# An attention and feed-forward kernel: the squares of the hidden values folded once more by GpSimd, their column sums moved behind the third up chunk

## Chip, cores and metric

One core of one Trainium2 chip. The metric is the device time of one launch in microseconds (us), lower is better. Matmuls run on TensorE (PE), element-wise work on VectorE (DVE), ScalarE (ACT) and GpSimd (POOL), transfers are issued by SyncE (SP). Each engine takes its instructions strictly in program order, and the engines meet at semaphores that the kernel writes out by hand.

## What is computed

Sixteen batch entries of 256 rows by 256 columns go through an attention block and then a ternary-weight feed-forward block, each with a layer norm before and after and a residual:

```
x = x + _layernorm(attn(_layernorm(x)))
x = x + _layernorm(ffn(_layernorm(x)))

def ffn(x):                      # FF = 1024 hidden columns
    gate, up = split(x @ wq_gate_up.T)
    h  = silu(gate) * up
    hn = h * rsqrt(mean(h * h, axis=-1) + eps)     # rms norm
    return hn @ wq_proj.T
```

The outer layer norm divides by the deviation of its input, so the kernel never applies the rms factor. It multiplies the un-normed `h` with the projection and adds a floor, worked out from the row sums of `h * h`, to the variance of the result. Those row sums are what the change is about.

## The kernel before

The attention part takes most of the program: until about 870 us, 128 steps of two heads. The feed-forward part follows, and its first steps lie between the last attention steps. Everything the change touches is in the feed-forward part.

A *unit* is one batch entry (256 rows, two tiles of 128). A *step* of the feed-forward pipeline works on five units at once, told by `FLAG = dict(stats=0, norm=1, turn=1, up=2, sum=3, down=3, z=3, out=4)`. Call w the unit whose `up` is in this step. Then the step holds

- the statistics of the input of unit w+2 (`stats_x2` on DVE, L1555 and L1558; `invert_x2` on POOL, four small operations, L620 to L627),
- the input norm of w+1 (`norm_x2` on ACT, L1175, two halves), its transposes on PE (L969), and the split of the result into a high part (`x2_hi`, ACT L1209) and a low part (`x2_lo`, DVE L1617),
- the up projection of w in four chunks c = 0 to 3 (`up`, PE L910, 16 matmuls each, gate half then up half). Each chunk goes through `activate` (silu, ACT L1154), `multiply` (gate times up, DVE L1535), `high_hidden` (ACT L1161), `square_hidden` (ACT L1168) and `split_hidden` (the low part, POOL L613),
- the down projection of w-1 (`down`, PE L940, 32 matmuls), the sums of its squares, the statistics of its result (`stats_z`, DVE L1582, L1587) and `invert_z` (four small POOL operations, L634 to L640),
- the outer norm of w-2 (`norm_z`, ACT L1183, two halves), its residual addition (`add_x`, POOL L646) and the store.

The squares of a unit are a tile of 8 slices of 128 hidden columns by 256 rows. DVE adds them down: `add_squares(0)` (L1542) brings slices 0 to 3 to two, `add_squares(2)` slices 4 to 7 to two, and `sum_squares` (L1548) the rest to slices 0 and 1. PE then multiplies slices 0 and 1 with a column of ones (`sum_tiles`, L920: for each of the two row tiles one matmul per slice, four in the program, eight rows in the trace), and DVE makes the floor of the sums (`sum_floor`, L1564).

The order of work is the order in which each engine's `step` function writes it. For PE that is up chunk 0, up chunk 1, down, sums, up chunk 2, transposes of w+1, up chunk 3. For POOL it is split 0, `invert_x2`, split 1, `add_x`, `invert_z`, split 2, split 3. The first of the four operations of `invert_x2` waits for two things:

```
pool.wait_ge(x2_aggr, u * 2 * NT + 2 * NT)
at_least(pool, x2_norm, u * NT)
```

Here u is w+2, so the second line asks that all units up to w+1 be normed by ACT: the small tiles of the statistics exist once and would be overwritten. `multiply` of chunk 3 stands behind `add_squares(0)` on DVE, and `multiply` of chunk 1 behind `add_squares(2)`, `sum_squares` and `stats_x2`.

The semaphores that matter: `h_summed` counts finished `sum_squares`, `sum_ready` finished sums on PE, `z_floored` finished floors, `x2_lo_done` lets the next unit's `up` begin.

Of the kernel before, what the change touches and what calls it, by code (L numbers as in the profile page):

```python
# [68 lines left out]
FC = 2  # L69
# [13 lines left out]
def sandwich_kernel(nc, x, wq, wkv, wkvh, wg, wout, wgu, wproj, rope, out):  # L83
    ctx = ExitStack()
    with ctx:
# [43 lines left out]
        def carve(*shape):  # L129
# [156 lines left out]
            sem(k) for k in ("h_added", "h_summed", "sum_ready", "z_floored", "z_ready"))  # L286
        z_stats, z_aggr, z_eps, z_neg, z_inv, z_biased, z_norm, res_done = (
            sem(k) for k in ("z_stats", "z_aggr", "z_eps", "z_neg", "z_inv", "z_biased", "z_norm", "res_done"))
        tile_done = sem("tile_done")
        stored = [sem(f"stored{i}") for i in range(2)]  # L290

        block = ctx.enter_context(nc.Block())
# [128 lines left out]
        def _(sp):  # L421
# [86 lines left out]
            sp.wait_ge(res_done, BATCH - 1)  # L508
            sp.dma_start(out_rows[:, TILES - 2 * NT:TILES - NT, :], res[0]).then_inc(stored[0], 16)
            for t in range(NT):  # L510
                sp.wait_ge(*((tile_done, t + 1) if t < NT - 1 else (res_done, BATCH)))
                sp.dma_start(out_rows[:, TILES - NT + t, :], res[1][:, t, :]).then_inc(stored[1], 16)
            sp.wait_ge(stored[0], 16 * BATCH // 2)
            sp.wait_ge(stored[1], 16 * BATCH // 2 + 16)
# [3 lines left out]
        def _(pool):  # L518
# [123 lines left out]
            def add_x(u, i):  # L642
# [2 lines left out]
                at_least(pool, stored[i], (u - i) * 8)  # L645
                nc.gpsimd.tensor_tensor(res[i], zn[i], x_batch(u), ALU.add).then_inc(res_done, 1)  # L646

            def place_down(g0, s):

                c = place_at(g0, s, PLACE_POOL)  # L650
                if c is not None:
                    j = c - (CHUNKS - ET)
                    pool.wait_ge(wt_back, 16 * CHUNKS)
                    pool.wait_ge(q_ready, STEPS)
                    nc.gpsimd.tensor_copy(wpr_t[:, :, j * P:(j + 1) * P],
                                          w_final[c].bitcast(BF16).rearrange("p (f c) -> p f c", c=P)).then_inc(wpr_placed, 1)

            def step(u0, s):
                at = unit_at(u0, s, FLAG["up"])
                if at:  # L660
                    split_hidden(*at, 0)
                at = unit_at(u0, s, FLAG["stats"])
                if at:
                    invert_x2(at[0])
                at = unit_at(u0, s, FLAG["up"])
                if at:
                    split_hidden(*at, 1)
                at = unit_at(u0, s, FLAG["out"])
                if at and not last_unit(at[0]):
                    add_x(*at)  # L670
                at = unit_at(u0, s, FLAG["z"])
                if at:
                    invert_z(*at)
                at = unit_at(u0, s, FLAG["up"])
                if at:
                    split_hidden(*at, 2)
                    split_hidden(*at, 3)

            def batch(g0, par, steps):
                for s in range(steps):  # L680
# [35 lines left out]
        def _(pe):  # L716
# [228 lines left out]
            def step(u0, s):  # L945
                at = unit_at(u0, s, FLAG["up"])
                if at:
                    up(*at, 0)
                at = unit_at(u0, s, FLAG["up"])
                if at:  # L950
                    up(*at, 1)
                at = unit_at(u0, s, FLAG["down"])
                if at:
                    u, i = at
                    down(u, i)
                    if not last_unit(u):
                        pe.wait_ge(h_summed, u + 1)
                        sum_tiles(u, i, range(FC))
                at = unit_at(u0, s, FLAG["up"])
                if at:  # L960
                    up(*at, 2)
                at = unit_at(u0, s, FLAG["turn"])
                if at:
                    u, i = at
                    pe.wait_ge(x2_norm, u * NT + NT)
                    at_least(pe, x2_lo_done, u)
                    for k in range(ET):
                        for t in range(NT):
# [50 lines left out]
        def _(act):  # L1019
# [164 lines left out]
                                         scale=z_rstd[:, t:t + 1]).then_inc(z_norm, 1)  # L1184

            def step(u0, s):
                at = unit_at(u0, s, FLAG["out"])
                if at:
                    norm_z(*at)
                at = unit_at(u0, s, FLAG["up"])  # L1190
                if at:
                    activate(*at, 0)
                    high_hidden(*at, 0)
                    activate(*at, 1)
                    high_hidden(*at, 1)
                at = unit_at(u0, s, FLAG["norm"])
                if at:
                    norm_x2(*at)
# [72 lines left out]
        def _(dve):  # L1271
# [295 lines left out]
            def add_x(u, i, t):  # L1567

                dve.wait_ge(z_norm, u * NT + t + 1)
                if t == 0:  # L1570
                    dve.wait_ge(stored[i], (u - i) * 8)
                nc.vector.tensor_tensor(res[i][:, t, :], zn[i][:, t, :], x_batch(u)[:, t, :], ALU.add)\
                    .then_inc(tile_done if t < NT - 1 else res_done, 1)

            def stats_z(u, i):

# [3 lines left out]
                at_least(dve, z_biased, u)  # L1580
                for t in range(NT):
                    nc.vector.bn_stats(z_stat[:, t, :], Z_BANK[i][:, t * E:(t + 1) * E]).then_inc(z_stats, 1)  # L1582
                if not last_unit(u):
                    sum_floor(u, i)
                dve.wait_ge(z_stats, u * NT + NT)
                for t in range(NT):
                    nc.vector.bn_aggr(z_agg[:, t, :], z_stat[:, t, :]).then_inc(z_aggr, 2)  # L1587
# [1 line left out]
            def step(u0, s):  # L1589
# [31 lines left out]
                if at:  # L1621
                    add_squares(*at, 0)
                    multiply(*at, 3)

            def batch(g0, par, steps):
                if isinstance(g0, int) and g0 == 0:
# [127 lines left out]
```

## Time and profile before

| | |
|---|---|
| median of 3 runs | 1093.43 us (1093.08 to 1095.97) |
| time of the profiled execution | 1093.13 us |
| its span | 1091.3 us |
| PE busy | 1052.3 us, 96% |
| POOL busy | 928.1 us, 85% |
| DVE busy | 872.8 us, 80% |
| ACT busy | 861.5 us, 79% |

The span is what the profiler saw between the first and the last instruction; the launch time is 1.8 us longer. Busy shares are means over the whole program. The feed-forward part has its own pattern, which repeats from unit to unit, and is read from a stretch or a timeline of its own. A busy PE in these rows counts a matmul from its start to its modelled end, so neighbouring matmuls overlap. "Idle before" in brackets is the time in which an engine had nothing, and the name behind it is what ended it.

### The profile page before, as it was taken

What the parts mean: (1) busy time and instruction counts of PE and PEld (TensorE: products, weight loads), DVE (VectorE), ACT (ScalarE), POOL (GpSimd) and SP (SyncE); (2) the same over time, 40 slices, a digit from 0 to 9 for tenths busy, and PEclk for the clock granted to TensorE, in tenths of its full rate; (3) what the DMA queues carried; (4) which work ended last, traced back from release to release, by engine and by line L of the source; (5) the groups of instructions that cost most, each with busy time, mean ns of one, the idle gap of its engine ahead of it and who ended that gap; (6) DMA issues with size and microseconds to landing.
All of it is one profiled execution on the core that took longest, in us unless ns stands there. A gap on an engine that the chain in (4) does not pass through costs nothing.

```text
span 1091.3 us, 25312 instructions
## 1 busy us (share of the span) xinstructions
PE 1052.3 (96%) x8010; PEld 1006.2 (92%) x8010; DVE 872.8 (80%) x2870; ACT 861.5 (79%) x2386; POOL 928.1 (85%) x846
## 2 busy tenths in 40 slices
PE   6899999999999999999999999999999899999997
PEld 6798999899989998998999999999999799999997
DVE  6879889989998998899889988987877656666654
ACT  4787888888888888887888788888878666666674
POOL 4698999899989999998999899999899658777685
PEclk9999999999999999999999999999999999999999
DMA  7450211021112110221021112111130000000001
GB/s 264 163 167 29 59 42 59 22 68 60 47 34 59 61 39 31 59 61 46 24 70 58 40 38 71 41 40 59 30 117 21 2 1 21 20 21 20 21 20 39
DMA packets 35124, 58.57 MB, mean 54 GB/s; under 512 B 3136, under 2 KB 16000, under 8 KB 34688
## 3 DMA queue, kind: packets, MB, share of 16 engines
q1 hardware_dynamic: 34992, 56.96, 16.6%
q8 instruction: 64, 1.05, 0.4%
q14 instruction: 68, 0.56, 0.2%
HBM read 50.92 MB, written 9.18 MB: 55 GB/s over the span
## 4 chain that ended last, share of the span: by engine, by line
POOL 59%; PE 21%; issue 17%; ACT 1%; DVE 1%; POOLq 0%; DMA 0%; ACTq 0%; DVEq 0%
POOL arena L575 15%; POOL arena L607 14%; POOL arena L596 14%; POOL arena L585 13%; PE psum L910 11%; PE psum L940 5%; PE psum L721 1%; PE psum L920 1%; PE psum L969 1%; POOL arena L545 1%; POOL X L566 1%; POOLq L297 0%; PE psum L747 0%; POOL arena L552 0%; PE psum L826 0%
## 5 line engine op out<-in xcount | busy, mean ns | idle before, releaser
L607 POOL TENSOR_TENSOR arena<-arena 128x768 f32<-128x768 f32 x128 | 196.5, 1535 | 18.8 <-DVE arena L1419 17.5
L575 POOL TENSOR_TENSOR arena<-arena,tables 128x512 f32<-128x512 f32 x128 | 165.7, 1295 | 39.4 <-ACT arena L1090 39.1
L585 POOL TENSOR_TENSOR arena<-arena 128x512 f32<-128x512 f32 x128 | 188.7, 1474 | 10.0
L1432 DVE SCALAR_TENSOR_TENSOR pt_split<-psum,vh_col,pt_split 128x256 fp32r<-128x256 f32 (+1 forms) x512 | 176.9, 407 | 0.0
L596 POOL TENSOR_TENSOR arena<-arena 128x512 f32<-128x512 f32 x128 | 165.2, 1290 | 2.6 <-DMA arena<-kh_rows 1.7
L826 PE MATMUL psum<-arena 128*128 128x256 f32 x512 | 154.6, 384 | 8.4 <-POOL arena L585 8.4
L1101 ACT ACTIVATE arena<-arena 128x256 f32<-128x256 f32 x256 | 128.6, 502 | 32.3 <-DVE arena L1409 25.5
L721 PE MATMUL psum<-wo_hi,o_hi 128*128 128x256 f32 x512 | 152.7, 298 | 0.0
L721 PE MATMUL psum<-xt_hi,wq_hi 128*128 128x256 f32 x512 | 146.0, 285 | 0.0
L721 PE MATMUL psum<-xt_lo,wq_hi 128*128 128x256 f32 x512 | 144.9, 283 | 0.0
L721 PE MATMUL psum<-xt_hi,wq_lo 128*128 128x256 f32 x512 | 144.9, 283 | 0.0
L721 PE MATMUL psum<-wo_hi,o_lo 128*128 128x256 f32 x512 | 144.2, 282 | 0.0
L721 PE MATMUL psum<-wo_lo,o_hi 128*128 128x256 f32 x512 | 143.7, 281 | 0.0
L721 PE MATMUL psum<-pt_split,vals_hi 128*128 128x512 f32 (+1 forms) x512 | 142.0, 358 | 0.4 <-DVE wo_lo L1283 0.4
L1089 ACT ACTIVATE arena<-psum 64x512 f32<-64x512 f32 x128 | 76.2, 596 | 80.9 <-DVE arena L1394 78.9
L910 PE MATMUL psum<-xt_hi,wq_hi 128*128 128x256 f32 x512 | 128.4, 290 | 0.5 <-DVE xt_lo L1617 0.5
L910 PE MATMUL psum<-xt_lo,wq_hi 128*128 128x256 f32 x512 | 124.6, 281 | 0.0
L1119 ACT ACTIVATE pt_split<-psum,vh_col 128x256 fp32r<-128x256 f32 x256 | 120.9, 472 | 0.0
L613 POOL TENSOR_TENSOR wo_lo<-arena,wo_hi 128x512 fp32r<-128x512 f32 x64 | 88.9, 1397 | 27.1 <-ACT wo_hi L1161 27.0
L828 PEld LDWEIGHTS psum<-arena 128*128 128x128 f32 x512 | 97.4, 190 | 13.5
L1441 DVE TENSOR_TENSOR o_lo<-psum,o_hi 128x512 fp32r<-128x512 f32 x128 | 87.2, 681 | 25.7 <-ACT o_hi L1129 25.6
L1407 DVE CUSTOM_DVE_ANT_0 arena<-psum,mask 128x256 f32<-128x256 f32 x256 | 106.8, 417 | 0.6 <-issue 0.5
(170 smaller groups left out, 3508.1 us busy)
## 6 DMA issues: line engine op xcount, KB each, us to landing
arena<-kh_rows SPq DMA_DIRECT2D x127, 256.0 KB, 3.3
out<-spare SPq DMA_DIRECT2D x15, 256.0 KB, 2.1
arena<-w_rows SPq DMA_DIRECT2D x6, 512.0 KB, 4.7
X<-L_attn_Wout SPq DMA_DIRECT2D x1, 2048.0 KB, 14.5
X<-L_attn_x SPq DMA_DIRECT2D x1, 2048.0 KB, 13.0
arena<-L_attn_Wq SPq DMA_DIRECT2D x1, 1536.0 KB, 10.1
X<-L_attn_x SPq DMA_DIRECT2D x1, 1536.0 KB, 10.2
w_rows<-L_ffn_w_gate_up SPq DMA_DIRECT2D x3, 512.0 KB, 9.3
```

The costliest lines, as they stand in the source:

```text
L575: nc.gpsimd.tensor_tensor(swap, swap, spread, ALU.mult).then_inc(q_sined, 1)
L585: nc.gpsimd.tensor_tensor(q_rot[p % 2], q_cos[p % 2], q_swap[p % 2], ALU.add).then_inc(q_roped, 1)
L596: nc.gpsimd.tensor_tensor(k_head[p % 2], keys[par].unsqueeze(1).to_broadcast([P, HP, N]), kh_all[p % 4], ALU.mult).then_inc(k_scaled, 1)
L607: nc.gpsimd.tensor_tensor(tb, tb, r.unsqueeze(3).to_broadcast([P, HP, 3, P]), ALU.mult).then_inc(p_ready, 1)
L721: last = nc.tensor.matmul(o, a, b, start=start and i == 0, stop=stop and i == len(passes) - 1, skip_group_check=skip)
L826: nc.tensor.matmul(sj[:, 0:2 * P], q[:, j, P:N], kt[:, j, :], start=True, stop=True, skip_group_check=True)
L828: nc.tensor.matmul(sj[:, 2 * P:3 * P], q[:, j, 0:P], kt[:, j, 0:P], start=False, stop=True, skip_group_check=True).then_inc(s_ready, 1)
L910: last = nc.tensor.matmul(bank[c % 2 * 2 + half][:, j * N:(j + 1) * N], wgu_t[:, k, col:col + P], part[:, k, :], start=n == 0 and j == 0, ...
L1101: nc.scalar.activation(tb[:, j, 0:2 * P], tb[:, j, 0:2 * P], ACT.Exp, scale=-1.0, bias=nmax[p % 4][:, 2 * j:2 * j + 1], accum_out=rsum[p % ...
L1119: nc.scalar.activation(pt_hi[p % 2][:, j * N:(j + 1) * N], b[:, 0:N], ACT.Copy, scale=vh[:, 0, h:h + 1])
L1407: nc.vector.tensor_tensor_reduce(tb[:, j, 0:2 * P], S_BANK[j][:, 0:2 * P], mask[:, :], -1.0, -MASKED, ALU.add, ALU.min, nmax[p % 4][:, 2 * ...
L1432: last = nc.vector.scalar_tensor_tensor(pt_lo[p % 2][:, o], b[:, i], vh[:, t, h:h + 1], pt_hi[p % 2][:, o].bitcast(F32), ALU.mult, ALU.sub ...
```

## The change

The diff does five things to the feed-forward steps.

1. POOL gets `fold_squares`: it adds slice 1 of the squares to slice 0 (128x256 numbers), for all units but the last, behind the low part of chunk 1. It waits for `h_summed` and counts `h_folded`.
2. PE sums slice 0 alone (two matmuls instead of four), no longer behind `down` but behind up chunk 2 and ahead of the transposes, and waits for `h_folded`.
3. POOL's `add_x` moves behind the low part of chunk 2, and `invert_z` to the end of the step, except for the last unit.
4. ACT's `norm_z` moves from the start of the step to behind `high_hidden` of chunk 1.
5. DVE's `sum_floor` moves from inside `stats_z` to the end of the step. The stores of the last unit wait for a semaphore of their own.

```diff
+            def fold_squares(u, i):
+
+                pool.wait_ge(h_summed, u + 1)
+                nc.gpsimd.tensor_tensor(squares[i][:, 0, :], squares[i][:, 0, :], squares[i][:, 1, :], ALU.add)\
+                    .then_inc(h_folded, 1)
...
                 at = unit_at(u0, s, FLAG["up"])
                 if at:
                     split_hidden(*at, 1)
+                at = unit_at(u0, s, FLAG["sum"])
+                if at and not last_unit(at[0]):
+                    fold_squares(*at)
+                at = unit_at(u0, s, FLAG["z"])
+                if at and last_unit(at[0]):
+                    invert_z(*at)
+                at = unit_at(u0, s, FLAG["up"])
+                if at:
+                    split_hidden(*at, 2)
                 at = unit_at(u0, s, FLAG["out"])
                 if at and not last_unit(at[0]):
                     add_x(*at)
+                at = unit_at(u0, s, FLAG["up"])
+                if at:
+                    split_hidden(*at, 3)
                 at = unit_at(u0, s, FLAG["z"])
-                if at:
+                if at and not last_unit(at[0]):
                     invert_z(*at)
-                at = unit_at(u0, s, FLAG["up"])
-                if at:
-                    split_hidden(*at, 2)
-                    split_hidden(*at, 3)
...
                     down(u, i)
-                    if not last_unit(u):
-                        pe.wait_ge(h_summed, u + 1)
-                        sum_tiles(u, i, range(FC))
                 at = unit_at(u0, s, FLAG["up"])
                 if at:
                     up(*at, 2)
+                at = unit_at(u0, s, FLAG["sum"])
+                if at and not last_unit(at[0]):
+                    u, i = at
+                    pe.wait_ge(h_folded, u + 1)
+                    sum_tiles(u, i, (0,))
...
-                at = unit_at(u0, s, FLAG["out"])
-                if at:
-                    norm_z(*at)
                 at = unit_at(u0, s, FLAG["up"])
                 if at:
                     activate(*at, 0)
                     high_hidden(*at, 0)
                     activate(*at, 1)
                     high_hidden(*at, 1)
+                at = unit_at(u0, s, FLAG["out"])
+                if at:
+                    norm_z(*at)
...
                     add_squares(*at, 0)
                     multiply(*at, 3)
+                at = unit_at(u0, s, FLAG["z"])
+                if at and not last_unit(at[0]):
+                    sum_floor(*at)
```

The change adds 17 lines, so a line behind the first of them has a higher number in the changed kernel. In the rows of the order below, L613 and L620 to L646 are the same in both; L910, L920, L940 and L969 of before are L924, L934, L954 and L985 of the changed kernel.

POOL, one step of the pipeline before, from `invert_x2` on:

```order
L620 TENSOR_TENSOR arena<-arena,eps 128x2 [waits x2_norm,x2_aggr]
L622 TENSOR_TENSOR arena<-arena 128x2
L624 TENSOR_TENSOR arena<-arena,minus_half 128x2 [waits x2_eps]
L627 TENSOR_TENSOR arena<-arena 128x2 [waits x2_inv,x2_neg]
L613 TENSOR_TENSOR wo_lo<-arena,wo_hi 128x512 [waits ht_hi_done]
L646 TENSOR_TENSOR spare<-arena,X 128x512 [waits stored1,z_norm]
L634 TENSOR_TENSOR arena<-arena 128x2 [waits z_norm,z_aggr,z_floored]
L635 TENSOR_TENSOR arena<-arena 128x2
L637 TENSOR_TENSOR arena<-arena,minus_half 128x2 [waits z_eps]
L640 TENSOR_TENSOR arena<-arena 128x2 [waits z_inv,z_neg]
L613 TENSOR_TENSOR wo_lo<-arena,wo_hi 128x512 [waits ht_hi_done] x3
```

The same place in the changed kernel (L651 is the fold):

```order
L620 TENSOR_TENSOR arena<-arena,eps 128x2 [waits x2_norm,x2_aggr]
L622 TENSOR_TENSOR arena<-arena 128x2
L624 TENSOR_TENSOR arena<-arena,minus_half 128x2 [waits x2_eps]
L627 TENSOR_TENSOR arena<-arena 128x2 [waits x2_inv,x2_neg]
L613 TENSOR_TENSOR wo_lo<-arena,wo_hi 128x512 [waits ht_hi_done]
L651 TENSOR_TENSOR arena<-arena 128x256 [waits h_summed]
L613 TENSOR_TENSOR wo_lo<-arena,wo_hi 128x512 [waits ht_hi_done]
L646 TENSOR_TENSOR spare<-arena,X 128x512 [waits stored0,z_norm]
L613 TENSOR_TENSOR wo_lo<-arena,wo_hi 128x512 [waits ht_hi_done]
L634 TENSOR_TENSOR arena<-arena 128x2 [waits z_norm,z_aggr,z_floored]
L635 TENSOR_TENSOR arena<-arena 128x2
```

The fold stands behind the whole of `invert_x2` and the low part of chunk 1, and `add_x` and `invert_z` have moved down.

PE before, the end of `down`, the sums and the start of up chunk 2:

```order
L940 MATMUL psum<-wq_lo,wo_hi 128x256
L940 MATMUL psum<-wq_lo,wo_lo 128x256
L920 MATMUL psum<-ones,arena 128x1 [waits z_floored,h_summed]
L920 MATMUL psum<-ones,arena 128x1 x3
L910 MATMUL psum<-xt_hi0,wq_hi 128x256 [waits gate_silu]
L910 MATMUL psum<-xt_lo0,wq_hi 128x256
```

PE in the changed kernel, the end of up chunk 2 up to the start of chunk 3:

```order
L924 MATMUL psum<-xt_lo0,wq_hi 128x256
L934 MATMUL psum<-ones,arena 128x1 [waits z_floored,h_folded]
L934 MATMUL psum<-ones,arena 128x1
L985 MATMUL psum<-ident,arena 128x128 [waits x2_lo_done,x2_norm]
L985 MATMUL psum<-ident,arena 128x128 x3
L924 MATMUL psum<-xt_hi0,wq_hi 128x256 [waits gate_silu]
L924 MATMUL psum<-xt_lo0,wq_hi 128x256
```

The sums are half as many, wait for another semaphore, and now stand directly ahead of the transposes.

## Rows read from the trace of the kernel before

**Rows 1.** Windows: busy time of each engine, granted clock, DMA share, GB/s.

```profile
980.00:1020.00 40.00, 40.00 (x332) 39.42 (x332) 25.02 (x53) 27.53 (x53) 28.60 (x40) 1.00 0.06 21
```

**Rows 2.** Chain that ended last, sums, up chunk 2, transposes: start us, us.

```profile
982.39 0.79 PE psum L920 x8
983.17 2.03 PE psum L910 x16
985.20 0.44 PE psum L969 x4
```

**Rows 3.** Waits, 900 to 1060 us: waiter, releaser, us in total, times, longest.

```profile
POOL arena L620 <- ACT arena L1175: 26.6, 12, 2.4
...
PEld psum L910 <- DVE xt_lo L1617: 2.9, 12, 0.5
```

**Rows 4.** Timeline, one step of the repeating pattern: start us, us, engine, line.

```profile
987.33 1.29 POOL L646 TENSOR_TENSOR spare<-arena,X 128x512 f32<-128x512 f32 x1
987.40 1.76 DVE L1542 TENSOR_TENSOR arena<-arena 128x512 f32<-128x512 f32 x1
...
989.08 0.67 DVE L1535 TENSOR_TENSOR arena<-arena,psum 128x512 f32<-128x512 f32 x1
...
989.79 0.63 ACT L1161 ACTIVATE wo_hi<-arena 128x512 fp32r<-128x512 f32 x1 [1.24 <-DVE arena L1535]
...
990.85 1.00 ACT L1183 ACTIVATE arena<-psum,arena 128x256 f32<-128x256 f32 x2
991.75 0.60 ACT L1154 ACTIVATE arena<-psum 128x512 f32<-128x512 f32 x1
992.38 0.69 DVE L1535 TENSOR_TENSOR arena<-arena,psum 128x512 f32<-128x512 f32 x1 [2.62 <-ACT arena L1154]
...
995.39 0.69 DVE L1535 TENSOR_TENSOR arena<-arena,psum 128x512 f32<-128x512 f32 x1
...
996.11 0.63 ACT L1161 ACTIVATE wo_hi<-arena 128x512 fp32r<-128x512 f32 x1 [1.90 <-DVE arena L1535]
996.65 1.08 ACT L1175 ACTIVATE arena<-X,arena 128x256 f32<-128x256 f32 x2
```

**Rows 5.** Timeline of POOL, next rows of the same step.

```profile
997.87 0.20 POOL L620 TENSOR_TENSOR arena<-arena,eps 128x2 f32<-128x2 f32 x1 [2.32 <-ACT arena L1175]
...
999.15 1.30 POOL L613 TENSOR_TENSOR wo_lo<-arena,wo_hi 128x512 fp32r<-128x512 f32 x1
1000.40 1.29 POOL L646 TENSOR_TENSOR spare<-arena,X 128x512 f32<-128x512 f32 x1
```

**Rows 6.** Timeline, step of unit 1, where `x2_hi` starts on an idle ACT.

```profile
892.29 0.19 POOL L634 TENSOR_TENSOR arena<-arena 128x2 f32<-128x2 f32 x1
...
892.42 0.60 PE L969 MATMUL psum<-ident,arena 128*128 128x128 f32 x4
...
893.06 0.60 ACT L1209 ACTIVATE xt_hi<-psum 128x512 fp32r<-128x512 f32 x1 [0.80 <-PE psum L969]
...
894.25 1.29 POOL L613 TENSOR_TENSOR wo_lo<-arena,wo_hi 128x512 fp32r<-128x512 f32 x1 [0.64 <-ACT wo_hi L1161]
894.29 1.80 DVE L1542 TENSOR_TENSOR arena<-arena 128x512 f32<-128x512 f32 x1
...
896.02 0.67 DVE L1535 TENSOR_TENSOR arena<-arena,psum 128x512 f32<-128x512 f32 x1
```

**Rows 7.** Groups by line and form, POOL: count, busy us, mean ns.

```profile
L637 POOL TENSOR_TENSOR arena<-arena,minus_half 128x2 f32<-128x2 f32 x16 | 11.2, 697 | 0.0
...
L552 POOL TENSOR_TENSOR arena<-arena 128x256 f32<-128x256 f32 x16 | 12.0, 748 | 1.6 <-DVE arena L1322 1.6
```

**Rows 8.** Windows, columns as in rows 1: a pause of PE, the end, a slow stretch.

```profile
854.00:858.00 4.00, 2.44 (x16) 2.08 (x15) 3.35 (x14) 1.98 (x7) 3.92 (x4) 1.00 0.00 0
1084.00:1088.00 4.00, 0.95 (x8) 0.74 (x7) 1.10 (x5) 0.40 (x1) 1.19 (x4) 0.82 0.10 33
22.00:24.00 2.00, 2.00 (x11) 2.00 (x10) 1.28 (x5) 0.00 (x0) 0.99 (x3) 0.50 0.70 169
```

More of the change, by code:

```diff
@@ L288, in sandwich_kernel @@
             sem(k) for k in ("z_stats", "z_aggr", "z_eps", "z_neg", "z_inv", "z_biased", "z_norm", "res_done"))
-        tile_done = sem("tile_done")
+        tile_done, h_folded = sem("tile_done"), sem("h_folded")
         stored = [sem(f"stored{i}") for i in range(2)]
@@ L510, in _ @@
             for t in range(NT):
-                sp.wait_ge(*((tile_done, t + 1) if t < NT - 1 else (res_done, BATCH)))
+                sp.wait_ge(tile_done, t + 1)
                 sp.dma_start(out_rows[:, TILES - NT + t, :], res[1][:, t, :]).then_inc(stored[1], 16)
@@ L667, in step @@
                     split_hidden(*at, 1)
-                at = unit_at(u0, s, FLAG["out"])
+                at = unit_at(u0, s, FLAG["sum"])
                 if at and not last_unit(at[0]):
-                    add_x(*at)
+                    fold_squares(*at)
                 at = unit_at(u0, s, FLAG["z"])
-                if at:
+                if at and last_unit(at[0]):
                     invert_z(*at)
@@ L676, in step @@
                     split_hidden(*at, 2)
+                at = unit_at(u0, s, FLAG["out"])
+                if at and not last_unit(at[0]):
+                    add_x(*at)
+                at = unit_at(u0, s, FLAG["up"])
+                if at:
                     split_hidden(*at, 3)
+                at = unit_at(u0, s, FLAG["z"])
+                if at and not last_unit(at[0]):
+                    invert_z(*at)
             def batch(g0, par, steps):
@@ L1186, in step @@
             def step(u0, s):
-                at = unit_at(u0, s, FLAG["out"])
-                if at:
-                    norm_z(*at)
                 at = unit_at(u0, s, FLAG["up"])
@@ L1195, in step @@
                     high_hidden(*at, 1)
+                at = unit_at(u0, s, FLAG["out"])
+                if at:
+                    norm_z(*at)
                 at = unit_at(u0, s, FLAG["norm"])
@@ L1572, in add_x @@
                 nc.vector.tensor_tensor(res[i][:, t, :], zn[i][:, t, :], x_batch(u)[:, t, :], ALU.add)\
-                    .then_inc(tile_done if t < NT - 1 else res_done, 1)
+                    .then_inc(tile_done, 1)
             def stats_z(u, i):
@@ L1582, in stats_z @@
                     nc.vector.bn_stats(z_stat[:, t, :], Z_BANK[i][:, t * E:(t + 1) * E]).then_inc(z_stats, 1)
-                if not last_unit(u):
-                    sum_floor(u, i)
                 dve.wait_ge(z_stats, u * NT + NT)
```

## Prediction

> **What bounds the kernel now.** The attention part is untouched by the change, so I start with the windows of the feed-forward part. PE is busy for all of 40 us at a granted clock of 1.00, while DVE, ACT and POOL are busy for 25 to 29 us [rows 1]. The chain that ended last says the same: it runs through nothing but PE, and per unit the sums cost 0.79 us, an up chunk 2.03 and the transposes 0.44 [rows 2]. By these two views alone, halving the sums would be a gain of 0.40 us per unit.
>
> The waits say that this is not all. In 160 us the load of the weights for an up chunk waited 12 times for `x2_lo` on DVE, 0.24 us each [rows 3]. So PE is full, yet it meets a loop of the other engines once per unit with almost no slack. In the timeline of one step [rows 4] that loop is nearly gapless: `add_squares(0)` at 987.40, `multiply` 3 at 989.08, the high part of chunk 3 at 989.79, `norm_z` at 990.85, silu 0 at 991.75, `multiply` 0 at 992.38, `multiply` 1 at 995.39, the high part of chunk 1 at 996.11, `norm_x2` at 996.65. From `norm_x2` it goes on to the squares, silu 2, `x2_hi`, `x2_lo` and the next up. One unit takes 13.07 us, from one `add_x` to the next (987.33 in rows 4, 1000.40 in rows 5); I use 13.08, since it lies between 13.07 and 13.09 from step to step.
>
> The third thing is a wait on an engine off the path. The first operation of `invert_x2` (L620) waited 26.6 us in 12 times for ACT's `norm_x2` [rows 3]; in one step 2.32 us of it, released when the norm that began at 996.65 for 1.08 us was done [rows 4, 5]. Before the change that wait costs nothing, since all that stands behind it on POOL is wanted late.
>
> **The change part by part.** *The sums.* Eight rows for 0.79 us become four, 0.40 us less of PE [rows 2].
>
> *The fold.* It adds 128x256 numbers on POOL. The same shape took 748 ns [rows 7], and I take 0.75. What matters is where it stands: behind `invert_x2` and the low part of chunk 1. L620 started at 997.87, the low part at 999.15, and what followed it at 1000.40 [rows 5]. The fold takes this last place and ends 0.75 us later. PE is done with up chunk 2 far earlier: chunk 2 ended at 985.20 in the chain of this kernel, where the fold of the same step would end at 988.1 (one period before 1000.40, plus 0.75), and without sums ahead of it 0.79 us sooner still. PE now stops at the sums until the fold is done, and behind them in its queue are the transposes of the next unit and up chunk 3. On the transposes hang `x2_hi`, `x2_lo` and `multiply` 3, and on these, through the loop above, the next `norm_x2` that lets `invert_x2` go. The wait feeds itself: a new loop closes over all five engines' queues.
>
> I add it up from start to start. From the transposes: to `x2_hi` 0.64 and on to `add_squares(0)` 1.23 [rows 6]; to `multiply` 3 1.73 [rows 6]; to the high part of chunk 3 0.71, through its square 1.06 (from 989.79 to 990.85, where `norm_z` stood and silu 0 now stands), to `multiply` 0 0.63, to `multiply` 1 3.01, to the high part of chunk 1 0.72 and to the place behind it 0.54 [rows 4]; there `norm_z`, 0.90 up to the next instruction (990.85 to 991.75), then `norm_x2` to L620 1.22, L620 to the low part 1.28, low part to fold 1.25 [rows 4, 5]; the fold 0.75 and 0.05 for the signal, and the four rows of sums 0.40. The sum is 0.64 + 1.23 + 1.73 + 0.71 + 1.06 + 0.63 + 3.01 + 0.72 + 0.54 + 0.90 + 1.22 + 1.28 + 1.25 + 0.80 + 0.40 = 16.12 us, 3.04 more than 13.08. It holds for the 12 steps w = 2 to 13, as many as there are waits of L620 in rows 3. That is 36.5 us.
>
> *The edges.* In the step of w = 1, PE is late for another reason: the place of the fold is 892.29 and the transposes began at 892.42 [rows 6]. With 0.80 for the fold and 0.40 for the sums they begin at 893.49, 1.07 us later. In the last two steps with a fold (w = 14 and 15) there are no statistics of a coming input, so L620 to L627 are not issued and the fold comes before PE is done with chunk 2. There the shorter sums count as a gain: up to 0.40 each, 0.7 in all.
>
> *`norm_z`* leaves the place ahead of silu 0 and goes ahead of `norm_x2`. Both places are in the loop, 0.90 us goes out and 0.90 comes in: nothing. If it had a free place, it would save 0.90. *`add_x` and `invert_z`* move behind work that waits for chunk 2 and 3. Who waits for them is `norm_z` of the next step, issued 8.4 us after `add_squares(0)`, and `invert_z` ends about 6 us after it: nothing, unless the port below interferes. *`sum_floor`* sits in a gap of DVE (2.62 us ahead of `multiply` 0 [rows 4]): nothing. The store of the last unit: nothing, between minus and plus 0.1.
>
> *Two prices that rows only bound.* First, the clock. PE will stand for some 3.7 us of each 16.1 (16.1 less 13.08 less the 0.40 of sums and the 0.24 of waits: 12.4 of work). After PE's last matmul the mean clock of four microseconds is 0.82 with 0.95 us of work in them, so it went from 1.00 to 0.50 about 1.4 us before their end; a stretch with 2.44 of 4 us busy stayed at 1.00 [rows 8]. The pauses to come lie between these, nearer to the first, so I expect falls to 1.2 GHz in most units. At that level 11 matmuls took 2.00 us, 0.18 each, against 332 in 40 us, 0.12 each [rows 1, 8]. An up chunk of 16 would end about 1 us later, and more if all of sums and transposes are slow too. `multiply` 3 has slack for it: its chunk is finished 0.44 + 2.03 us behind the start of the transposes, while `add_squares(0)` lets `multiply` 3 go only after 3.60. So a fall costs between 0 and 1.2 us per unit. I take 0.5, since it is rarely the whole stretch: 6.0 us in 12 units.
>
> Second, the port between DVE and POOL. `add_squares(0)` reads both operands from SBUF, as POOL's work does. It began at 894.29, 0.04 us after POOL's low part at 894.25, and took 1.80 us; it took 1.76 behind `add_x` [rows 4, 6]. In the new loop the pair of rows 6 returns in every unit, and its 1.73 is in my sum. If DVE came first, 1.1 us would go, down to where PE's chunk 3 is the limit (2.47 against 3.60). That is the lower bound of this term; the upper is the rival below.
>
> The Trainium skill says in "SBUF — State Buffer", section "Who interferes with whom", that a DVE instruction with two SBUF inputs and a reading GpSimd instruction exclude one another, and that whoever issues first keeps the ports for its whole instruction. The trace agrees for the wide operations: 1.80 us behind a start only 0.04 us earlier. By the same rule the small operations of `invert_z` would block as well, which no row here shows; that is the second rival.
>
> **Sum.** 1093.13 (the profiled execution, 0.3 below the median of the runs) + 36.5 + 1.07 - 0.7 + 6.0 = 1136.0 us.
>
> **Rivals.** *POOL takes the port in two more places.* `invert_z` now comes behind the low part of chunk 3, that is 2.6 to 4 us after `multiply` 3, and `add_squares(2)` of the next unit starts 3.0 us after `multiply` 3 (0.71 + 1.06 + 0.63 + 0.60). The power operation of `invert_z` takes 0.70 us [rows 7] and could hold the port; then the low part of chunk 0 may get in ahead of `sum_squares`. That is 0.66 plus 1.1 us, 1.75 per unit: 12 x 1.75 = 21 more, 1157 us. For it speaks that the times fall on one another within 0.1 us; against it that such a small operation reads two numbers per partition and need not hold a port for its full 0.70.
>
> *The cheap form of the wait.* The clock stays up and DVE wins the port: the period is 16.12 less 1.09 = 15.03, and the time 1093.13 + 12 x 1.95 + 1.07 - 0.7 = 1116.9. For it: the race in rows 6 was decided by 0.04 us. Against it: it went to POOL in rows 6, where `x2_hi` started on an idle ACT as it will now. With only the clock up it is 1130.
>
> *The fold is ready when PE comes, and the kernel gets faster.* Its data are there in time: `sum_squares` lies before `multiply` 1. Then `add_squares(0)` meets a fold of 0.75 instead of an `add_x` of 1.29, 0.55 less, and PE has 0.40 less work and no wait of 0.24; both loops come to about 12.5 us. Over 14 units that is 14 x 0.55 = 7.7 us less, 1085.4. It decides at the end of `norm_x2`: L620 would have to be released nearly 4 us earlier than in rows 5. Against it stand the 12 waits of rows 3, which name `norm_x2`, and POOL's strict order.
>
> **Chances.** The forecast, the wait behind `invert_x2` with some units at the lower clock: 0.60, by itself 1129 to 1144. The port rival: 0.17. The cheap form, wholly or in part: 0.17. Fold in time and faster: 0.04. Gain and wait cancelling: 0.02. The range from 1117 (cheap form) to 1157 (port) leaves out little more than the faster side. About 0.3% (3.3 us) is what a measurement of this kernel tells from no change: faster by more 0.04, within it 0.02, slower by more 0.94.
>
> **What would show it.** In the profile after: PE waits about 12 times for POOL at the sums, 3 to 4 us each, 40 us or so in all; the chain that ended last leaves PE and runs through ACT, DVE and POOL; the unit takes 16 to 17 us; the windows of the feed-forward part show PE at 75 to 80% and a clock between 0.8 and 1.0; `add_squares(0)` stays near 1.8 us. Wrong would be: no wait of PE for the fold; a unit near 15 us (then the port went the other way); one near 18 with `add_squares(2)` or `sum_squares` over 0.69 us (the port rival); a clock of 1.00 throughout (the 6 us fall away).

## The result, and the profile after

The changed kernel takes 1142.84 us, median of 4 runs (1141.98 to 1146.07), against 1094.7 for the kernel before in the same session (1093.08 to 1095.98): a ratio of 1.044 [1.042, 1.0459], 48 us slower. The forecast was 1136.0, with a range of 1117 to 1157. The profiled execution took 1141.98 us, its span is 1140.2, 48.9 more than before.

The engines' busy times and shares on the page of the changed kernel:

```profile
PE 1062.3 (93%) x7950; PEld 1016.1 (89%) x7950; DVE 877.9 (77%) x2870; ACT 862.6 (76%) x2386; POOL 938.2 (82%) x861
```

A share of 93% still looks like a kernel bound by PE. It is an average over stages, and in the busy time of PE there are matmuls that run at half the clock. The same 40 us of the feed-forward part as in [rows 1], of the changed kernel:

```profile
980.00:1020.00 40.00, 34.28 (x246) 33.88 (x247) 19.98 (x38) 21.09 (x40) 23.98 (x32) 0.87 0.04 14
```

PE is busy for 34.28 us instead of 40.00, at a mean clock of 0.87 instead of 1.00, and does 246 matmuls instead of 332. No other engine works more than before; each is busy for less time. So nothing became a bound by being full. The waits of 900 to 1110 us (waiter, releaser, us in total, times, longest) say what it is:

```profile
ACT xt_hi L1225 <- PE psum L985: 41.4, 12, 3.9
...
PEld psum L934 <- POOL arena L651: 39.9, 12, 6.9
...
POOL arena L620 <- ACT arena L1191: 36.8, 12, 4.9
```

PE's load for the sums (L934) waited 12 times for the fold (L651), 39.9 us in all; in the kernel before, PE's loads waited 2.9 us, and for another engine [rows 3]. The wait of L620 for `norm_x2` grew from 26.6 to 36.8 us. The chain that ended last (start us, us, what), once around the loop:

```profile
996.53 0.69 POOL arena L651
997.26 0.61 PE psum L934 x4
997.87 0.70 PE psum L985 x4
998.57 3.05 PE psum L924 x15
...
1001.89 0.70 DVE arena L1551
...
1003.15 0.61 ACT arena L1184
...
1004.28 0.69 DVE arena L1551
...
1007.31 0.70 DVE arena L1551
...
1008.57 1.01 ACT arena L1199 x2
1009.58 0.99 ACT arena L1191 x2
...
1011.04 0.65 POOL arena L624
1011.83 0.20 POOL arena L627
1012.03 1.22 POOL wo_lo L613
1013.24 0.69 POOL arena L651
```

Where [rows 2] were nothing but PE, the chain now goes from the fold to the sums and transposes, over up chunk 3, `multiply` 3, silu 0, `multiply` 0 and 1, `norm_z` (L1199), `norm_x2` (L1191), `invert_x2` and the low part of chunk 1 back to the next fold, 16.71 us later (996.53 to 1013.24).

One row of it stands out. Up chunk 3 took 3.05 us; a chunk took 2.03 before [rows 2]. The windows (columns as in [rows 1]) around it in the changed kernel:

```profile
994.00:998.00 4.00, 1.40 (x13) 1.20 (x12) 0.69 (x1) 1.37 (x3) 3.06 (x6) 1.00 0.00 0
998.00:1001.00 3.00, 3.00 (x17) 3.00 (x16) 1.77 (x2) 1.80 (x4) 1.20 (x1) 0.50 0.00 0
...
1002.00:1006.00 4.00, 4.00 (x36) 4.00 (x35) 2.33 (x5) 2.63 (x5) 3.31 (x6) 1.00 0.21 70
```

PE stood until the sums began at 997.26. Just behind them, at 998.0, the clock fell from 2.4 to 1.2 GHz, stayed there for some 3 us of full work, and rose again.

The timeline of the same step holds the race for the port between DVE and POOL:

```profile
999.80 1.28 POOL L613 TENSOR_TENSOR wo_lo<-arena,wo_hi 128x512 fp32r<-128x512 f32 x1 [2.59 <-ACT wo_hi L1177]
999.84 1.78 DVE L1558 TENSOR_TENSOR arena<-arena 128x512 f32<-128x512 f32 x1
...
1004.86 0.70 POOL L637 TENSOR_TENSOR arena<-arena,minus_half 128x2 f32<-128x2 f32 x1
1004.88 0.71 DVE L1558 TENSOR_TENSOR arena<-arena 128x512 f32<-128x512 f32 x1
1005.63 0.69 DVE L1564 TENSOR_TENSOR arena<-arena 128x512 f32<-128x512 f32 x1
1005.70 0.68 POOL L640 TENSOR_TENSOR arena<-arena 128x2 f32<-128x2 f32 x1
```

POOL's low part wins by 0.04 us, as in [rows 6], and `add_squares(0)` takes 1.78 us. At 1004.86 the power operation of `invert_z` is ahead of `add_squares(2)` by 0.02 us, and DVE takes 0.71 us, 0.03 more than alone: it was hardly held up. A small operation waits instead: the last of `invert_z` (L640), begun 0.07 us behind `sum_squares` (L1564), takes 0.68 us, and 0.20 alone.

**The 48.9 us of span, by the starts of `add_squares(0)`.** The pieces are differences to the kernel before, in us. From w = 1 to w = 13 the changed kernel needs 204.63 us (895.34 to 1099.97), before 158.53 (894.29 to 1052.82).

| piece | measured | forecast |
|---|---|---|
| step of w = 1 | +1.05 | +1.07 |
| w = 1 to 13, eleven of the twelve | 11 x (16.77 - 13.13) = +40.1 | 11 x 3.54 = +38.9 |
| w = 3 to 4 | 20.11 - 14.09 = +6.0 | +3.5 |
| w = 13 to 15 | 24.07 - 24.41 = -0.3 | -0.7 |
| from there to the end | 16.16 - 14.07 = +2.1 | 0 |

### The profile page after: what moved, and what is told of

It is laid out like the page before. It is cut to its first block, busy times and chain, and to the rows that moved or that the text cites. A ratio compares the mean times of both kernels' runs of the same rounds, so it can differ in the third digit from the quotient of the medians.

```text
span 1140.2 us, 25207 instructions
## 1 busy us (share of the span) xinstructions
PE 1062.3 (93%) x7950; PEld 1016.1 (89%) x7950; DVE 877.9 (77%) x2870; ACT 862.6 (76%) x2386; POOL 938.2 (82%) x861
## 3 DMA queue, kind: packets, MB, share of 16 engines
q8 instruction: 64, 1.05, 0.4%
## 4 chain that ended last, share of the span: by engine, by line
POOL 60%; issue 18%; PE 11%; DVE 5%; ACT 4%; POOLq 0%; DMA 0%; ACTq 0%; DVEq 0%; SPq 0%
POOL arena L575 14%; POOL arena L607 14%; POOL arena L596 14%; POOL arena L585 12%; PE psum L924 6%; DVE arena L1551 2%; POOL wo_lo L613 1%; ACT arena L1191 1%; PE psum L735 1%; PE psum L934 1%; PE psum L954 1%; ACT arena L1199 1%; PE psum L985 1%; DVE arena L1558 1%; DVE arena L1571 1%
## 5 line engine op out<-in xcount | busy, mean ns | idle before, releaser
L575 POOL TENSOR_TENSOR arena<-arena,tables 128x512 f32<-128x512 f32 x128 | 165.6, 1293 | 40.1 <-ACT arena L1106 39.7
L735 PE MATMUL psum<-xt_hi,wq_hi 128*128 128x256 f32 x512 | 146.0, 285 | 0.0
L735 PE MATMUL psum<-xt_lo,wq_hi 128*128 128x256 f32 x512 | 144.8, 283 | 0.0
L924 PE MATMUL psum<-xt_hi,wq_hi 128*128 128x256 f32 x512 | 137.4, 301 | 0.0
L924 PE MATMUL psum<-xt_lo,wq_hi 128*128 128x256 f32 x512 | 135.0, 300 | 0.0
L613 POOL TENSOR_TENSOR wo_lo<-arena,wo_hi 128x512 fp32r<-128x512 f32 x64 | 84.4, 1319 | 54.9 <-ACT wo_hi L1177 54.6
```

The costliest lines, as they stand in the source:

```text
L575: nc.gpsimd.tensor_tensor(swap, swap, spread, ALU.mult).then_inc(q_sined, 1)
L735: last = nc.tensor.matmul(o, a, b, start=start and i == 0, stop=stop and i == len(passes) - 1, skip_group_check=skip)
L924: last = nc.tensor.matmul(bank[c % 2 * 2 + half][:, j * N:(j + 1) * N], wgu_t[:, k, col:col + P], part[:, k, :], start=n == 0 and j == 0, ...
```

## The experiments

Eleven kernels ran. Each ratio is to the kernel before.

**Is it the place of the fold behind `invert_x2`?** `e1_fold_early` moves the fold on POOL ahead of `invert_x2` and leaves the rest as changed:

```diff
                     split_hidden(*at, 0)
+                at = unit_at(u0, s, FLAG["sum"])
+                if at and not last_unit(at[0]):
+                    fold_squares(*at)
                 at = unit_at(u0, s, FLAG["stats"])
...
                     split_hidden(*at, 1)
-                at = unit_at(u0, s, FLAG["sum"])
-                if at and not last_unit(at[0]):
-                    fold_squares(*at)
```

> The changed kernel with one edit: the fold stands on POOL directly behind the low part of chunk 0, ahead of invert_x2, instead of behind invert_x2 and the low part of chunk 1. Theory A (the fold's place behind invert_x2, which waits for norm_x2, closes a loop over all queues): PE no longer waits at the sums, the unit falls from 16.8 us to about 12.5 us (PE's own work: 13.08 less 0.40 of sums less the 0.24 of wait), 1083 to 1090 us. Theory B (the extra work on POOL, the fold's hold on the port and the moved add_x and invert_z are what costs): the same work is still there, the time stays above 1120 us.

Measured 1087.76 us, ratio 0.9944 [0.9926, 0.9962]. Its waits of 950 to 1050 us no longer have a row for the fold; what is left for PE is this:

```profile
PEld psum L924 <- DVE xt_lo L1631: 1.9, 8, 0.2
```

And its window is full again, at full clock:

```profile
980.00:1020.00 40.00, 39.92 (x333) 39.29 (x332) 24.18 (x55) 28.90 (x57) 32.27 (x46) 1.00 0.06 21
```

The unit takes 12.63 us. One addition of 0.7 us, put ahead of `invert_x2` and the low part of chunk 1 instead of behind them, is worth 55 us. With the fold there, the whole change is a small gain of 0.6%.

`e3_stats_behind_fold` asks which of the two things ahead of the fold it is. It keeps the fold behind the low part of chunk 1 and puts `invert_x2` behind it:

```diff
-                at = unit_at(u0, s, FLAG["stats"])
-                if at:
-                    invert_x2(at[0])
                 at = unit_at(u0, s, FLAG["up"])
...
                     fold_squares(*at)
+                at = unit_at(u0, s, FLAG["stats"])
+                if at:
+                    invert_x2(at[0])
```

> The changed kernel with invert_x2 moved behind the fold: POOL does low 0, low 1, fold, invert_x2, low 2, add_x, low 3, invert_z. The fold still waits behind the low part of chunk 1, but no longer behind norm_x2. Theory A: the chain through the fold is then 9.73 + 0.70 + 1.25 + 0.80 + 0.40 = 12.9 us per unit with add_squares(0) blocked and about 11.8 without, so PE or the loop of ACT and DVE is the bound again: 12.5 to 13.0 us per unit, 1085 to 1093 us, PE's wait for the fold under 1 us per unit. A rival by which the place behind the low part of chunk 1 alone is the cause: PE still waits 3 us and the time stays above 1120 us.

Measured 1094.33, ratio 1.0006 [0.9992, 1.002]. Between 950 and 1050 us PE hardly waits for the fold:

```profile
PEld psum L934 <- POOL arena L651: 1.3, 6, 0.2
```

So the large wait comes from `invert_x2` and its release by `norm_x2`, not from the low part. The total is 1.3 us above the range that I expected. The later units take 12.63 us as in `e1_fold_early`. The early ones are slower, above all the steps of w = 3 and 4, where PE still waits for the fold (905 to 945 us):

```profile
PE psum L934 <- POOL arena L651: 6.2, 3, 3.4
```

In `e1_fold_early` this row reads 0.8 us. In these steps POOL also has the residual additions of the last attention batches (L566), and in that of w = 4 one of them takes the port ahead of `add_squares(2)`:

```profile
927.32 1.30 POOL L566 TENSOR_TENSOR X<-X,arena 128x512 f32<-128x512 f32 x1
927.35 1.82 DVE L1558 TENSOR_TENSOR arena<-arena 128x512 f32<-128x512 f32 x1
```

The low part of chunk 1 comes later with it, and the fold behind it. The place behind the low part is thus early enough in the settled units only.

`e2_no_fold` takes the fold out and lets PE sum both slices in the new place, on `h_summed`:

```diff
-                    pe.wait_ge(h_folded, u + 1)
-                    sum_tiles(u, i, (0,))
+                    pe.wait_ge(h_summed, u + 1)
+                    sum_tiles(u, i, range(FC))
```

> The changed kernel without the fold: PE sums both slices (eight rows again), waits for h_summed as before, but in the new place behind up chunk 2; the other moves stay. Theory A: no wait, PE-bound with 12.85 us per unit, about 1090 us (1086 to 1094). Theory B, if the moves of add_x, invert_z and norm_z are to blame: above 1110 us. The difference to e1 is what the shorter sums are worth where PE is the bound: 0.40 us per unit, 5 us in all; if another engine is then the bound, less.

Measured 1091.2, ratio 0.9972 [0.9961, 0.9984], as expected. It is 3.4 us above `e1_fold_early`, with some 2.4 us either way. That is what the fold is worth when it is in time: 0.23 us in each of 15 folds, against 0.40 of PE's work taken away.

**What does the clock cost?** `e4_fill_pause` puts 22 matmuls into a spare bank ahead of PE's wait, so that PE does not stand:

```diff
                     u, i = at
+                    for n in range(22):
+                        nc.tensor.matmul(F_BANK[:, 0:N], wgu_t[:, 0, 0:P], x2_hi[i][:, 0, :], start=True, stop=True,
+                                         skip_group_check=True)
                     pe.wait_ge(h_folded, u + 1)
```

> The changed kernel with 22 extra matmuls of 128x256 on PE (2.6 us at full speed, their result is overwritten by the transposes) ahead of its wait for the fold, so that PE works through most of the pause. It tells what the lower TensorE clock costs. Theory A: the granted clock stays at 1.00, the unit goes from 16.8 to about 16.1 us, the sum of the chain by rows of before; 1142 less 12 x 0.65 = 1134 us (1132 to 1137), although PE does 2.6 us more per unit. If the clock costs nothing: 1142 us or more.

Measured 1144.4, ratio 1.0447 [1.0429, 1.0466], not the gain expected. The settled units (from w = 5 on) did what they should: the clock is 1.00 and `add_squares(0)` starts each 16.19 us in its timeline (L1561, since the edit adds three lines):

```profile
985.64 1.80 DVE L1561 TENSOR_TENSOR arena<-arena 128x512 f32<-128x512 f32 x1
...
1001.83 1.80 DVE L1561 TENSOR_TENSOR arena<-arena 128x512 f32<-128x512 f32 x1
```

But the extra matmuls also stood in the three steps without a long pause (w = 1, 14 and 15), 2.6 us of work each. `e10_fill_where_idle` leaves them out there:

```diff
-                    for n in range(22):
+                    for n in range(22 if isinstance(u, int) and 1 <= u <= 12 else 0):
```

> As e4, but the 22 extra matmuls stand only in the twelve steps w = 2 to 13, where PE pauses. In e4 the unit was 16.19 us in a row at a clock of 1.00, against 16.77 on average in the changed kernel, but the same matmuls also stood in the steps of w = 1, 14 and 15, where PE has no pause, 3 x 2.6 us. So this kernel should show the price of the lower clock in its time: 12 x 0.58 = 7 us less than 1142.8, 1134 to 1138 us. If e4's time was not due to those three steps: 1142 us or more.

Measured 1135.47, ratio 1.0376 [1.0359, 1.0394]: the clock costs 0.0064 of 1094 us, 7 us with some 3 either way. The traces say it more sharply. The 16.77 us of the changed kernel are a mean of eleven steps, the 16.19 those of the settled ones, so the two do not compare. From w = 1 to w = 13 `e10_fill_where_idle` needs 198.64 us (897.85 to 1096.49) against 204.63, that is 6.0 us, or 0.50 a step. One fall of the clock is left in it, in the step of w = 4. Its window:

```profile
1020.00:1040.00 20.00, 19.04 (x160) 18.84 (x160) 11.56 (x25) 10.49 (x20) 13.06 (x19) 1.00 0.07 21
```

PE is busy for 95% of these 20 us at full clock, some of it with work that nobody uses, and the kernel is still 3.8% slower than before.

**What does the port cost?** `e11_fill_port_order` is `e10_fill_where_idle` with POOL's low part of chunk 2 held back until `add_squares(0)` is done, so that DVE goes first:

```diff
+                if c == 2:
+                    pool.wait_ge(h_added, 2 * u + 1)
                 pool.wait_ge(ht_hi_done, u * (FT // FC) + (c + 1))
```

> As e10, and POOL starts the low part of chunk 2 only when add_squares(0) is done (a wait on h_added), so that DVE takes the port first. It tells the price of the blocked add_squares(0) in the new loop. By the prediction's lower bound 1.1 us of it shows where the clock is up: the unit falls from 16.19 to 15.1 us and the time by 12 x 1.1 = 13 us against e10, 1120 to 1126 us; add_squares(0) takes 0.68 us. The rival: the low parts behind it on POOL come later and block add_squares(2) and sum_squares instead; then these take more than 0.69 us and the gain is under 5 us.

Measured 1127.85, ratio 1.0319 [1.0298, 1.0341]: a gain of 7.6 us, short of the 13 expected. Its timeline (L1563 is `add_squares`, L615 the low part):

```profile
991.01 0.68 DVE L1563 TENSOR_TENSOR arena<-arena 128x512 f32<-128x512 f32 x1
...
994.28 1.29 POOL L615 TENSOR_TENSOR wo_lo<-arena,wo_hi 128x512 fp32r<-128x512 f32 x1
...
994.75 1.36 DVE L1563 TENSOR_TENSOR arena<-arena 128x512 f32<-128x512 f32 x1
```

`add_squares(0)` takes 0.68 us, as it does without POOL beside it. But now `add_squares(2)` starts 0.47 us behind a low part of POOL (994.28) and takes 1.36. The unit is 15.90 instead of 16.19. Of the 7.6 us, 3.1 are that the long unit at w = 3 to 4 is gone too (16.18 instead of 19.30).

**What is the place of `norm_z` worth?** `e5_norm_back` is the changed kernel with `norm_z` at the start of ACT's step, where it was before:

```diff
             def step(u0, s):
+                at = unit_at(u0, s, FLAG["out"])
+                if at:
+                    norm_z(*at)
```

> The changed kernel with ACT's norm_z put back to the start of the step. Theory A: norm_z lies in the closed loop in both places (ahead of silu 0, or between the high part of chunk 1 and norm_x2), so the unit stays at 16.1 us plus what the clock costs, and the time within 2 us of the changed kernel, 1141 to 1145 us. The rival, that the move of norm_z ahead of norm_x2 is what makes invert_x2 and with it the fold late: 12 x 0.90 = 11 us less, 1132 us.

Measured 1180.4, ratio 1.0779 [1.0748, 1.0811]: a large miss. The waits of 950 to 1050 us have a row that the changed kernel does not have:

```profile
ACT arena L1199 <- POOL arena L640: 10.8, 5, 2.2
```

And in its timeline:

```profile
998.85 1.28 POOL L613 TENSOR_TENSOR wo_lo<-arena,wo_hi 128x512 fp32r<-128x512 f32 x1 [0.20 <-ACT wo_hi L1177]
...
1001.22 0.20 POOL L640 TENSOR_TENSOR arena<-arena 128x2 f32<-128x2 f32 x1
1001.45 1.02 ACT L1199 ACTIVATE arena<-psum,arena 128x256 f32<-128x256 f32 x2 [2.16 <-POOL arena L640]
1002.36 0.59 ACT L1170 ACTIVATE arena<-psum 128x512 f32<-128x512 f32 x1
```

`invert_z` now stands behind the low part of chunk 3 (998.85) and ends at 1001.4. `norm_z` waits 2.16 us for it in front of silu 0, and the whole loop waits with it. From w = 1 to w = 13 a step takes 19.61 us on average against 17.05, so this wait is most of the 2.56 more. By this trace the move of `norm_z` is what lets `invert_z` stand so late; a kernel with `norm_z` and `invert_z` both back was not run.

`e6_norm_gap` puts `norm_z` of the changed kernel between silu 1 and the high part of chunk 1, where ACT waits for DVE anyway:

```diff
                     activate(*at, 1)
-                    high_hidden(*at, 1)
                 at = unit_at(u0, s, FLAG["out"])
                 if at:
                     norm_z(*at)
+                at = unit_at(u0, s, FLAG["up"])
+                if at:
+                    high_hidden(*at, 1)
```

> The changed kernel with norm_z between silu 1 and the high part of chunk 1, where ACT sat idle for 1.92 us waiting for multiply 1. Theory A: its 0.90 us leave the loop, the unit falls from 16.8 to about 15.9 us, 12 x 0.9 = 11 us less: 1132 us (1129 to 1135). If the loop does not run through ACT between multiply 1 and norm_x2: 1142 us.

Measured 1127.99, ratio 1.031 [1.0286, 1.0334], 1 us below the range expected. From w = 4 to 13 the unit takes 15.46 us where the changed kernel takes 16.68, so 1.2 less, more than the 0.90 that the sum gives for `norm_z`; the clock was higher too (0.982 against 0.977 over the program), which would fit the rest.

`e7_before_norm_gap` makes the same move in the kernel before.

> The kernel before the change with one edit: norm_z between silu 1 and the high part of chunk 1. It tells how much of the 13.08 us of a unit was the loop of ACT and DVE. If that loop holds PE up by 0.24 us per unit, as PE's waits for x2_lo say, PE's work alone remains: 12.85 us, 3 us less in all, 1091 us. If PE alone was the bound: 1094 us, no change.

Measured 1102.07, ratio 1.0063 [1.0039, 1.0087]: slower, where a gain was expected. Its timeline (L1544 is `add_squares`, L1550 `sum_squares`):

```profile
983.84 1.34 DVE L1544 TENSOR_TENSOR arena<-arena 128x512 f32<-128x512 f32 x1
...
984.67 1.66 POOL L613 TENSOR_TENSOR wo_lo<-arena,wo_hi 128x512 fp32r<-128x512 f32 x1
...
985.22 1.67 DVE L1550 TENSOR_TENSOR arena<-arena 128x512 f32<-128x512 f32 x1
```

Silu 0 comes 0.9 us earlier, and with it `add_squares(2)` and `sum_squares`, which now run beside POOL's low parts and take 1.34 and 1.67 us instead of 0.68 each. That loses 1.65 and wins 0.90, 0.75 in sum, and the unit grows by 0.71, from 13.08 to 13.79.

**The best version.** `e8_early_norm_gap` has the fold early and `norm_z` in the gap (the edits of `e1_fold_early` and `e6_norm_gap` together).

> The fold behind the low part of chunk 0 (as in e1) and norm_z between silu 1 and the high part of chunk 1: both loops have slack, PE's work is the bound. e1 had 12.62 us per unit; PE's work without any wait is 13.08 less 0.24 less 0.40 = 12.44. Theory A: at most 0.2 us less per unit than e1, 1085 to 1088 us. If e1 was still held by the loop of ACT and DVE the gain is larger, up to 12 x 0.9 us, but PE has no room for it.

Measured 1085.96, ratio 0.9915 [0.9892, 0.9938], faster than both kernels; against `e1_fold_early` (0.9944) the intervals overlap. PE is full without a gap in these 40 us:

```profile
980.00:1020.00 40.00, 40.00 (x340) 40.00 (x339) 25.26 (x56) 29.97 (x58) 34.05 (x47) 1.00 0.06 21
```

`e9_before_fold_early` adds the early fold alone to the kernel before, with the sums of one slice at their old place behind `down`:

```diff
-                        pe.wait_ge(h_summed, u + 1)
-                        sum_tiles(u, i, range(FC))
+                        pe.wait_ge(h_folded, u + 1)
+                        sum_tiles(u, i, (0,))
```

> The kernel before with the fold alone: POOL folds behind the low part of chunk 0, PE sums one slice and waits for the fold, but at the old place behind down. It tells whether the move of the sums behind up chunk 2 is needed. In the trace of before the low part of chunk 0 ended at 982.47 and the sums began at 982.22; the fold would end at 983.2, so PE waits 1.0 us and saves 0.40. Theory A: about 0.4 us more per unit than 13.08, 1095 to 1101 us. If the shorter sums were worth more than the wait: under 1092 us.

Measured 1097.4, ratio 1.0029 [1.0014, 1.0045], as expected. At the old place PE still waits for the fold (950 to 1050 us):

```profile
PEld psum L929 <- POOL arena L651: 4.4, 7, 0.7
```

So with the sums at their old place the early fold brings no gain. 0.85% of the time, some 9 us, lie between this kernel and `e1_fold_early`; the latter has the other moves too, and their share was not measured.

## Why the prediction was right

**The loop.** The sum of starts gave 16.12 us per unit with the clock up and the port lost. `e4_fill_pause` and `e10_fill_where_idle`, with the clock up and the port lost, measure 16.19 in their settled units. The 12 waits of PE for POOL, 39.9 us, are the "40 us or so" of the forecast. That the wait behind `invert_x2` closes the loop is shown by `e1_fold_early` and `e3_stats_behind_fold`, which take the fold out from behind it in two ways. One sign missed: PE was to be busy for 75 to 80% of a window and was for 86% (34.28 of 40 us). The sum put its pause at 3.7 us. With the clock up that is about right: in `e10_fill_where_idle` 22 matmuls of 0.12 us and a wait of 0.96 fill it, 3.6 in all. At the lower clock PE's own work takes longer, and in the settled units of the changed kernel the pause was 2.1 to 3.6 us. The forecast lies 6.0 us below the profiled execution, and the table above says where: 1.1 in the eleven steps, 2.5 in the step of w = 4, 0.4 at w = 14 and 15 and 2.1 at the end.

**The edges.** In the step of w = 1 the forecast was 1.07 us, and 1.05 came. The gain at w = 14 and 15 was 0.3 instead of 0.7. Behind them 2.1 us were lost that the prediction did not have. One part is the clock: at the last down chunk the changed kernel's windows read

```profile
1130.00:1132.00 2.00, 2.00 (x16) 2.00 (x16) 0.16 (x1) 1.00 (x2) 0.00 (x0) 0.78 0.02 4
1132.00:1134.00 2.00, 0.96 (x5) 0.66 (x4) 0.90 (x4) 0.00 (x0) 0.00 (x0) 0.50 0.00 0
```

where the fall in [rows 8] came behind PE's last matmul. From the floor of the last sums to the statistics it took 1.82 us (1131.18 to 1133.00) instead of 1.06. Another is DVE's last residual addition beside the late `add_x` of POOL, in the timeline of the changed kernel:

```profile
1135.51 1.26 POOL L646 TENSOR_TENSOR spare<-arena,X 128x512 f32<-128x512 f32 x1
...
1136.19 1.20 DVE L1588 TENSOR_TENSOR spare<-arena,X 128x256 f32<-128x256 f32 x2 [2.08 <-ACT arena L1199]
```

Before it took 0.88. "`add_x` moves: nothing" was 0.3 us wrong here, by the port that the prediction had made its condition. The rest is in the timelines too. PE began the last down projection 1.50 us behind the last `add_squares(0)` instead of 1.06. And the program ended 2.8 us behind the last addition instead of 2.2: the store of unit 14, which waits for the late `add_x`, is issued at 1136.80, directly ahead of the last two stores, which would fit.

**The clock.** Its direction was right, and its size was 0.50 us a step by the experiments, where 0.5 stood. That the two agree so well is partly luck. The slack that I gave `multiply` 3 (1.1 us) was too large: it set a length on the chain (0.44 and 2.03) against starts in the timeline. The transposes start at 997.73 and stand on the chain from 997.87, and `multiply` 3 starts 0.27 us behind the end of chunk 3. That leaves 0.7 us, and the fall costs 1.3: up chunk 3 took 1.0 us more, and the transposes ahead of it 0.70 us instead of 0.44. So `multiply` 3 starts 4.16 us behind the transposes (997.73 and 1001.89) instead of the 3.60 of the sum. The forecast took the fall as "rarely the whole stretch"; in this step it covered chunk 3 almost whole. Against that it came in only nine of the twelve steps. PE's waits ahead of these nine were 2.49 to 6.65 us long; in the other three (w = 3, 10 and 12) they were 2.29, 2.12 and 2.10, and the clock stayed at 1.00:

```profile
1046.80 0.38 PE L934 MATMUL psum<-ones,arena 128*128 128x1 f32 x2 [2.12 <-POOL arena L651]
```

**The port.** The sum takes POOL to be first at `add_squares(0)` in every unit, and so it was (1.78 to 1.80 us each). The Trainium skill says in "SBUF — State Buffer", section "Who interferes with whom", that a DVE instruction with two SBUF inputs and a reading GpSimd instruction exclude one another for the whole instruction. For the wide ones the trace agrees (1.78 us against 0.68 in `e11_fill_port_order`); for the 128x2 operations it does not: 0.70 to 0.72 us in nine units, begun 0.02 to 0.04 us behind one of 0.70. So the rival that small operations of `invert_z` hold the port falls. What it feared happened once, by a wide operation, in the step of w = 4:

```profile
935.43 1.30 POOL L566 TENSOR_TENSOR X<-X,arena 128x512 f32<-128x512 f32 x1
935.45 1.82 DVE L1558 TENSOR_TENSOR arena<-arena 128x512 f32<-128x512 f32 x1
...
936.69 1.74 POOL L613 TENSOR_TENSOR wo_lo<-arena,wo_hi 128x512 fp32r<-128x512 f32 x1
937.31 1.66 DVE L1564 TENSOR_TENSOR arena<-arena 128x512 f32<-128x512 f32 x1
```

L566 is the residual addition of the last attention batch. It is ahead of `add_squares(2)` by 0.02 us, then the low part of chunk 0 gets in ahead of `sum_squares`: 1.14 and 0.98 us, 2.1 of the 2.5 that this unit is above the forecast, if all of it lies on the path.

**`norm_z`.** "0.90 goes out and 0.90 comes in: nothing" treated as separate what is one thing. Taken back alone, the move costs 37.6 us (`e5_norm_back`). For the pair as changed the sum, which holds 0.90 us for `norm_z`, came out; by itself it was not measured.

**The rival "fold in time".** It was right in what it would bring: a unit of "about 12.5 us" and 1085.4 us against 12.63 and 1087.76 in `e1_fold_early`. It was right too that L620 decides it, though its step at the port did not come so: `add_squares(0)` met no POOL work and took 0.68 us, and `add_squares(2)` took 1.23.

## What to carry to other kernels

Before an instruction that another engine waits for is queued on an engine with idle time, read what the instructions ahead of it in that queue wait for. An idle wait costs nothing until something urgent stands behind it; here one place in the queue decided between -6 and +48 us. The period of such a loop can be summed from the starts in one timeline of the kernel before, and came out to within 0.1 us here, for the units at full clock.

A slot won by a shift is not a gain yet where two engines share a port: in `e7_before_norm_gap` and `e11_fill_port_order` the operations moved out of one collision into the next.

## What the runs showed of the hardware

A wide DVE addition (128x512) that started beside a wide POOL addition took up to 1.84 us instead of 0.68, and a start 0.02 us later was enough. It ended some 0.55 us behind POOL's (1001.62 and 1001.08; 937.27 and 936.73). A 128x2 operation of POOL did not hold DVE up by more than 0.04 us, but was held up by it (0.68 against 0.20).

When DVE waited for the port and POOL had another operation queued behind the one that ran, DVE was next, in all fourteen such meetings of the changed kernel: `add_squares(0)`, begun at 999.84 behind the low part of 999.80 to 1001.08, ended at 1001.62, and POOL's `add_x`, begun at 1001.03, took 1.74 us instead of 1.29.

In the changed kernel nine pauses of PE of 2.49 to 6.65 us, one in a unit of some 16.8, were followed by a clock of 1.2 GHz; three of 2.10 to 2.29 us were not. The clock fell inside three of the pauses (3.57 to 6.65 us) and up to 1.6 us after work had begun again behind the others (998.0 behind 997.26). It stayed down for some 3 us six times and some 7 us three times. The price fell on the first chunk behind the pause (3.05 us instead of 2.03), which is on the path.
